# The three-layer feature-crossing tower, staged anew: 32 rounds of 512 columns, and VectorE's share of the low parts contracted in full fp32

## The chip, the core and the metric

One core of one Trainium2 chip runs the whole program. The metric is the device time of one execution in microseconds (us); lower is better. Engines are named as in the profile: PE is TensorE, DVE is VectorE, ACT is ScalarE, POOL is GpSimd, SP is the queue that issues most DMAs.

## The reference

For 1024 rows, 39 table lookups give `e` of 39 fields x 16 numbers. Three layers follow, each over the products of the 39 fields with the state of the layer before (39 fields for layer 0, then 64 rows), and a small dense network on top:

```python
for i, (W, b) in enumerate(zip(Ws, bs)):          # W0: 39*39 x 128; W1, W2: 39*64 x 128
    z = jnp.einsum('bfd,bgd->bfgd', x, h)
    cur = jax.nn.relu(jnp.einsum('bfgd,fgl->bld', z, Wr) + b[None, :, None])
    if i != n - 1:
        h = cur[:, :L // 2]
        direct = cur[:, L // 2:]
    else:
        direct = cur
    outs.append(direct)
return jnp.concatenate(outs, axis=1).sum(-1)
...
h = jnp.maximum(h @ W_top1 + b_top1, 0.0)         # 272 -> 512, with 16 dense columns
h = jnp.maximum(h @ W_top2 + b_top2, 0.0)         # 512 -> 256
y = h @ W_top3
```

All of it is fp32. There are 1024 x 16 = 16384 columns (row, d) in all. Layer 0 uses its symmetry: with the weights of (f,g) and (g,f) added, only 20 cyclic shifts of the fields are needed, three shifts (117 rows) to a tile, which makes 7 tiles. Layers 1 and 2 have 39 x 64 products, which is 19.5 tiles of 128 rows.

## The kernel before

The columns are taken in 16 steps of 1024 (128 batch rows x 8 values of d; `HD`, `N`, `NST`). A unit of work is one tile of 128 (or 117) products by 1024 columns. Its life is: DVE multiplies (`product`, L484 for layers 1 and 2 with h in PSUM and the replicated fields `xr` in SBUF; L474 for layer 0 with both operands in SBUF; L489 for the last half tile), then PE contracts it (`contract`, L712) in one of three ways that `KINDS0` and `KINDS1` write out:

- F: full fp32, two 512-column matmuls, each shown as two records in the profile.
- G: split. ACT copies z to `zh` in fp32r (`hi`, L583), POOL makes `zl = z - zh` (`subtract`, L269), and PE makes three passes of two matmuls each: wl x zh, wh x zh, wh x zl.
- D: the same, but DVE makes `zl` (L502), two units behind its own product (`LAG_SUB`).

A round is layer 0 (7 tiles) of one step, layer 2 (20) and layer 1 (20), 47 units: 20 F, 17 G, 10 D. Two rounds handle one block of 128 rows; PE, DVE, ACT, POOL and SP each run this order in a loop of their own, bound by counting semaphores. The z ring has 6 slots, zh has 5, zl has 3. The half tile of layers 1 and 2 (L723) is done as two 64-row matmuls in different halves of the array.

SP reloads everything replicated from the transposed inputs `xT` in memory: `xk` and `xs` for layer 0 (L359, L364), `xr` and `xl` for layers 1 and 2 (L371, L374), packets of 4 KB. POOL also gathers the embeddings (L255, 39 per block, L252 the ids). PE transposes them (L700), ACT copies the result out and writes `xT` (L594, L598). Sums over d are DVE's (`sum_d`, L511, L515). ACT also makes the relus (`take0`, `take1`, `take2`, L602). The dense network is at the end (`top`, L803, 14 groups), four of its groups before the last layer 2.

## Time and profile before

| | |
|---|---|
| time, median of 3 runs | 1478.6 us (1478.53 to 1479.51) |
| the profiled execution, from its first to its last instruction | 1477.0 us |
| PE matmul busy | 1256.5 us (85%) |
| DVE busy | 1289.5 us (87%) |
| POOL busy | 1052.5 us (71%) |
| ACT busy | 616.3 us (42%) |
| data moved by DMA | 240.57 MB, 163 GB/s |

The profile has no other time for its execution than its span; the runs lie 1.6 us above it in the median, which is what stands outside the first and last instruction. Busy shares are averages over the span, and PE's records overlap in time, so PE's real rate has to be taken from start to start.

### The profile page before, as it was taken

The numbers are of one execution on the slowest core, as the hardware profiler recorded it, in microseconds if no ns is written. First come the engines' busy times: TensorE is split into PE (matmuls) and PEld (weight loads), VectorE is DVE, ScalarE is ACT, GpSimd is POOL, SyncE is SP. The second block draws the span as 40 slices with busy tenths as digits, with TensorE's granted clock in tenths as the row PEclk, the third lists the DMA queues.
The fourth block names the chain that finished last, engine by engine and source line by source line (L and its number), as shares of the span: only waits on it lengthen the run. The fifth ranks groups of instructions, "written<-read, shape, count | busy, mean of one in ns | idle before, by whom it ended". The sixth has DMA issues, their size and how long they took to land.

```text
span 1477.0 us, 15917 instructions
## 1 busy us (share of the span) xinstructions
PE 1256.5 (85%) x4096; PEld 726.8 (49%) x4096; DVE 1289.5 (87%) x1021; ACT 616.3 (42%) x639; POOL 1052.5 (71%) x598
## 2 busy tenths in 40 slices
PE   0057899899988999899988899889988999999999
PEld 0024555455545555455545455555545556555653
DVE  0056989999899999999899999999899999999970
ACT  2122444335353443435443453435444354445442
POOL 6668578885889668894889659895788756555550
PEclk9999999999999999999999999999999999999999
DMA  5189794958769393967949395875949497888600
GB/s 147 21 211 216 169 227 122 212 139 194 179 148 222 100 230 115 210 165 161 223 113 219 100 226 155 175 189 128 227 122 214 123 206 187 176 200 182 136 25 1
DMA packets 89021, 240.57 MB, mean 163 GB/s; under 512 B 21542, under 2 KB 30871, under 8 KB 88888
## 3 DMA queue, kind: packets, MB, share of 16 engines
q1 hardware_dynamic: 77446, 233.70, 67.9%
q0 software_dynamic: 10240, 2.74, 1.7%
q10 hardware_dynamic: 1312, 3.87, 0.9%
q8 instruction: 9, 0.15, 0.0%
q14 instruction: 14, 0.11, 0.0%
HBM read 235.46 MB, written 7.14 MB: 164 GB/s over the span
## 4 chain that ended last, share of the span: by engine, by line
issue 36%; DVE 29%; PE 11%; DMA 7%; POOL 7%; SPq 6%; ACT 2%; DVEq 1%; POOLq 0%; ACTq 0%
DVE z L484 17%; PE curA L712 7%; DVE zl L502 6%; POOL zl L269 5%; DVE z L474 4%; DMA idx<-in_ids_dram 3%; POOL emb L255 2%; SPq L371 2%; DMA xr<-xT 2%; DMA xl<-xT 2%; PE h L803 2%; DVE part L511 1%; PE curB L712 1%; SPq L352 1%; SPq L355 1%
## 5 line engine op out<-in xcount | busy, mean ns | idle before, releaser
L269 POOL TENSOR_TENSOR zl<-z,zh 128x1024 fp32r<-128x1024 f32 (+1 forms) x272 | 668.4, 2459 | 288.9 <-ACT zh L583 263.9
L583 ACT ACTIVATE zh<-z 128x1024 fp32r<-128x1024 f32 (+1 forms) x432 | 455.2, 1058 | 723.0 <-DVE z L484 461.0
L484 DVE TENSOR_TENSOR z<-xr,h 128x1024 f32<-128x1024 f32 x608 | 705.1, 1210 | 53.5 <-PE curA L712 17.7
L255 POOL DMA_INDIRECT emb<-in_tbl_dram,idx x312 | 378.9, 1215 | 97.1 <-issue 61.3
L712 PE MATMUL curA<-z,wf 128*128 128x512 f32 (+1 forms) x592 | 283.4, 601 | 28.6 <-issue 25.3
L502 DVE TENSOR_TENSOR zl<-z,zh 128x1024 fp32r<-128x1024 f32 (+1 forms) x160 | 293.9, 1837 | 5.1 <-ACT zh L583 4.4
L712 PE MATMUL curB<-z,wf 128*128 128x512 f32 (+1 forms) x560 | 267.8, 601 | 4.7 <-DVE z L484 4.7
L712 PE MATMUL curA<-zl,wh 128*128 128x512 f32 (+1 forms) x438 | 148.4, 420 | 70.7 <-POOL zl L269 56.8
L474 DVE TENSOR_TENSOR z<-xk,xs 117x1024 f32<-117x1024 f32 x112 | 193.1, 1773 | 14.3 <-DMA xs<-xT 14.3
L712 PE MATMUL curA<-zh,wl 128*128 128x512 f32 (+1 forms) x438 | 188.2, 511 | 1.4 <-ACT zh L583 1.4
L712 PE MATMUL curB<-zl,wh 128*128 128x512 f32 (+1 forms) x426 | 143.3, 418 | 53.4 <-POOL zl L269 43.8
L712 PE MATMUL curB<-zh,wl 128*128 128x512 f32 (+1 forms) x426 | 182.6, 510 | 1.5 <-ACT zh L583 1.4
L712 PEld LDWEIGHTS curA<-z,wf 128*128 128x128 f32 (+1 forms) x592 | 110.8, 190 | 130.0 <-issue 103.5
L712 PEld LDWEIGHTS curB<-z,wf 128*128 128x128 f32 (+1 forms) x560 | 105.1, 191 | 97.8 <-issue 76.7
L712 PE MATMUL curA<-zh,wh 128*128 128x512 f32 (+1 forms) x438 | 137.1, 394 | 0.0
L712 PEld LDWEIGHTS curA<-zl,wh 128*128 128x128 f32 (+1 forms) x438 | 74.1, 188 | 125.9 <-POOL zl L269 95.7
L712 PE MATMUL curB<-zh,wh 128*128 128x512 f32 (+1 forms) x426 | 133.0, 393 | 0.0
L712 PEld LDWEIGHTS curB<-zl,wh 128*128 128x128 f32 (+1 forms) x426 | 72.2, 188 | 103.7 <-POOL zl L269 78.2
L712 PEld LDWEIGHTS curA<-zh,wl 128*128 128x128 f32 (+1 forms) x438 | 81.8, 190 | 79.1 <-issue 55.3
L712 PEld LDWEIGHTS curB<-zh,wl 128*128 128x128 f32 (+1 forms) x426 | 79.8, 190 | 72.1 <-issue 54.2
L712 PEld LDWEIGHTS curA<-zh,wh 128*128 128x128 f32 (+1 forms) x438 | 82.5, 188 | 18.6
L712 PEld LDWEIGHTS curB<-zh,wh 128*128 128x128 f32 (+1 forms) x426 | 80.2, 188 | 18.4
(60 smaller groups left out, 432.6 us busy)
## 6 DMA issues: line engine op xcount, KB each, us to landing
xr<-xT SPq DMA_DIRECT2D x288, 512.0 KB, 9.3
xs<-xT SPq DMA_DIRECT2D x112, 468.0 KB
xr<-xT SPq DMA_DIRECT2D x32, 256.0 KB
xk<-xT SPq DMA_DIRECT2D x16, 468.0 KB
emb<-in_tbl_dram,idx POOLq DMA_INDIRECT x312
xl<-xT SPq DMA_DIRECT2D x32, 128.0 KB
xT<-direct ACTq DMA_DIRECT2D x16, 156.0 KB
xT<-direct ACTq DMA_DIRECT2D x16, 80.0 KB
```

Of the source, the lines that this page charges most:

```text
L255: nc.gpsimd.indirect_dma_start(out=emb[:, f * D:(f + 1) * D], out_offset=None, in_=tables[f], in_offset=bass.IndirectOffsetOnAxis(ap=idx[: ...
L269: nc.gpsimd.tensor_tensor(zl[0:r, q, :], z[0:r, slot(i), :], zh[0:r, h, :], ALU.subtract).then_inc(lo_pool, 1)
L352: sp.dma_start(stage[0][k:R0:K, t, :], cols).then_inc(w0_loaded, 16)
L355: sp.dma_start(w0t[k:R0:K, t, :], rows).then_inc(w0_loaded, 16)
L371: sp.dma_start(xr[par * H:par * H + H, 2 * q:2 * q + n, :], src).then_inc(xr_loaded[q], 16)
L474: nc.vector.tensor_tensor(z[0:R0, slot(i), :], xk[0:R0, :], xs[0:R0, r, :], ALU.mult).then_inc(z_ready, 1)
L484: ins = nc.vector.tensor_tensor(z[:, slot(i), :], xr[:, t, :], h[:, :], ALU.mult)
L502: nc.vector.tensor_tensor(zl[0:r, q, :], z[0:r, slot(i), :], zh[0:r, h, :], ALU.subtract).then_inc(lo_dve, 1)
L511: nc.vector.tensor_reduce(part[:] if half else zs[:, which, :], src[:].rearrange("p (d b) -> p b d", d=HD), AX.X, ALU.add).then_inc(sum_do ...
L583: nc.scalar.activation(zh[0:r, split_slot(kinds, i, HI_RING), :], z[0:r, slot(i), :], ACT.Copy).then_inc(hi_ready, 1)
L712: mm = nc.tensor.matmul(cur[:, b * BK:(b + 1) * BK], w[0:r, :], v[0:r, b * BK:(b + 1) * BK], start=start_, stop=stop_)
L803: mm = nc.tensor.matmul(cur[0:w.shape[1], cols], w, v, start=(q == 0), stop=(q == len(parts) - 1))
```

## The change

The whole body is rewritten. What it does:

- The columns go in 32 steps of 512 (128 rows x 4 values of d). A unit is now a pair of tiles by 512 columns, so it still has 1024 columns for DVE, ACT and POOL. A round has 24 units: 10 of layer 1, 10 of layer 2 and 4 of layer 0 (the last with one tile), for three different steps. There are 29 full rounds, three before them that lack layers, two after them without layer 0, and a last one with layer 2 alone.
- `KINDS` has F and G only: 15 F (one of them of half size) and 9 G a round. D is used in the rounds before round 0 alone. The half tile is now a second tile of an F unit, with 64 rows: unit 9 ends with it in layer 1, unit 10 begins with it in layer 2, in the other half of the array.
- h is kept in PSUM in two arrangements side by side (`take` makes 6 relus instead of 2), so that one replicated tile `xr` serves two tiles of products: 9 x 256 KB and 512 KB of `xq` are loaded a step, in 14 DMAs of packets of 2 KB.
- For layer 0 the left operand `xk` is no longer loaded: PE transposes the embeddings, copied three times side by side by ACT (`copy_emb`), straight into PSUM (`turn`), where DVE reads it with a stride (`product0`). All of `xs` for a step comes in three DMAs and has one buffer.
- Rings: z 8, zh 4, zl 4. Two embedding buffers. SP writes `xT`. ACT's order inside a round has waits for PE: `take2` at unit 0, `copy_xc` (which waits for `turn` behind PE's unit 1) at unit 2.
- The sums over d stay in SBUF (`zq`, `zs`). Seven of the eight blocks of rows go through the dense network before the last round; the last block follows at the end with 128 columns.

```diff
+DQ = 4
+N = DQ * P
+STEPS = B * D // N
...
+KINDS = "GFGFFGFGFF" + "FGFGFFGFGF" + "FGFF"
+UNITS = len(KINDS)
+A_END, C_END = 10, 20
+FIRST, LAST = -3, STEPS - 1
+LOOP = 8
+LOOPED = (1, 25)
+NZ, NH, NL = 8, 4, 4
...
+def kind(r, u):
+    k = KINDS[u]
+    return "D" if k == "G" and r < 0 else k
...
+            def load_xs(t):
+                for k in range(K):
+                    nt = T0 if k < 2 else T0 - 1
+                    src = bass.AP(xT.tensor, (t * XR + k) * N, [[N, F], [K * N, T0], [1, N]])
+                    sp.dma_start(xs[k * F:(k + 1) * F, :].rearrange("p (t c) -> p t c", c=N), src).then_inc(xs_loaded, 16)
+
+            def load_xr(t, slot, k):
+                for a in range(4):
+                    src = bass.AP(xT.tensor, (t * XR + 12 * k + a) * N, [[0, Q], [4 * N, 3], [1, N]])
+                    sp.dma_start(xr[slot][a * Q:(a + 1) * Q, 3 * k * N:3 * (k + 1) * N].rearrange("p (q c) -> p q c", c=N),
+                                 src).then_inc(xr_loaded[slot][k], 16)
...
+            def round_(r, j=0):
+                t = r + 3
+                if t < STEPS:
+                    sp.wait_ge(xc_copied, t + 1 + LOOP * j)
+                    sp.nop(nofuse=True)
+                    write_x(t + LOOP * j, t % 2)
+                    sp.wait_ge(xT_written[t % 2], 32 * (t // 2 + 1) + 16 * LOOP * j)
+                    sp.nop(nofuse=True)
+                    sp.wait_ge(z_ready, NUM[r - 1, UNITS - 1] + 1 + ZU * j)
+                    sp.nop(nofuse=True)
+                    load_xs(t + LOOP * j)
+                t = r + 2
+                if t < STEPS:
+                    sp.wait_ge(z_ready, NUM[r, A_END] + 1 + ZU * j)
+                    sp.nop(nofuse=True)
+                    load_xq(t + LOOP * j, t % 2)
+                    for k in range(3):
+                        sp.wait_ge(z_ready, NUM[r, A_END + 3 * k + 3] + 1 + ZU * j)
+                        sp.nop(nofuse=True)
+                        load_xr(t + LOOP * j, t % 2, k)
+
...
+            def product1(r, u, j):
+                s = r + 1
+                if u == 0:
+                    dve.wait_ge(read0, 7 * (s + 1) + RU * j)
+                z_free(r, u, j)
+                if u < NQ:
+                    if u % 3 == 0:
+                        dve.wait_ge(xr_loaded[s % 2][u // 3], 64 * (s // 2 + 1) + 32 * LOOP * j)
+                    x = xr[s % 2][:, u * N:(u + 1) * N].unsqueeze(1).to_broadcast([P, 2, N])
+                    pair(x, h1[:, :].rearrange("p (a n) -> p a n", a=2), z_slot(r, u)).then_inc(z_ready, 1)
...
+            def product0(r, u, j):
+                s = r + 3
+                if u == C_END:
+                    dve.wait_ge(turned, s + 1 + LOOP * j)
+                    dve.wait_ge(xs_loaded, 48 * (s + 1) + 48 * LOOP * j)
+                z_free(r, u, j)
+                t = 2 * (u - C_END)
+                nt = tiles_of(u)
+
+                x = xk_bank(s)[0:R0, :].rearrange("p (d b) -> p b d", d=DQ).unsqueeze(1).to_broadcast([R0, nt, P, DQ])
+                nc.vector.tensor_tensor(
+                    z[0:R0, z_slot(r, u), 0:nt * N].rearrange("p (a b d) -> p a b d", a=nt, d=DQ), x,
+                    xs[0:R0, t * N:(t + nt) * N].rearrange("p (a b d) -> p a b d", a=nt, d=DQ),
+                    ALU.mult).then_inc(z_ready, 1)
...
+            def copy_xc(t, j):
+                act.wait_ge(turned, t + 1 + LOOP * j)
+                if t >= 2:
+                    act.wait_ge(xT_written[t % 2], 32 * (t // 2) + 16 * LOOP * j)
+                nc.scalar.activation(xc[t % 2][:, :].rearrange("p (b d) -> p b d", d=DQ),
+                                     xk_bank(t)[0:F, :].rearrange("p (d b) -> p b d", d=DQ), ACT.Copy).then_inc(xc_copied, 1)
...
+            def take(i, h, cur, bias, done, to):
+
+                if i < 2:
+                    relu(h[i * H:(i + 1) * H, 0:N], cur[0:H, :], bias[0:H, :], done)
+                elif i < 6:
+                    p, f = (i - 2) * Q, (i - 1) % 2 * Q
+                    relu(h[p:p + Q, N:2 * N], cur[f:f + Q, :], bias[f:f + Q, :], done)
...
+            def round_(r, j=0):
+                if r == -2:
+                    for i in range(7):
+                        take0(r, i, j)
+                for u in range(UNITS):
+                    if present(r, u):
+                        hi(r, u, j)
+                    if u == 0 and r >= 1:
+                        take2(r - 1, j)
+                    if u == 0 and r >= 1 and (r + 3) % PER_B == 0 and r <= STEPS - 4:
+                        copy_emb((r + 3) // PER_B, j)
+                    if u == 2 and 0 <= r <= STEPS - 4:
+                        copy_xc(r + 3, j)
+                    if u == A_END - 1 and r == -1:
+                        for i in range(7):
+                            take0(r, i, j)
...
+                        take0(r, u - 11, j)
+                    if 0 <= r <= STEPS - 4 and u >= C_END:
+                        for i in range(2 * (u - C_END), min(7, 2 * (u - C_END) + 2)):
+                            take1(r, i, j)
+                    if u == UNITS - 1 and (r == -1 or STEPS - 4 < r <= STEPS - 2):
...
+            def turn(t, b, j):
+
+                ev = emb[b % 2][:, :].rearrange("p (f d) -> p d f", d=D)
+                for c in range(DQ):
+                    mm = nc.tensor.transpose(xk_bank(t)[0:R0, c * P:(c + 1) * P], ev[:, DQ * (t % PER_B) + c, :],
+                                             ident[:, :])
+                mm.then_inc(turned, 1)
+
+            def contract(r, u, j, cur, start, stop):
+                n = tiles_of(u)
+                if kind(r, u) == "F":
+                    pe.wait_ge(z_ready, NUM[r, u] + 1 + ZU * j)
+                    order = (1, 0) if u == A_END else range(n)
+                    for i, a in enumerate(order):
+                        rows = rows_of(u, a)
+                        mm = nc.tensor.matmul(cur[:, :], wf[rows, full_at(u), a, :],
+                                              z[rows, z_slot(r, u), a * N:(a + 1) * N],
+                                              start=start and i == 0, stop=stop and i == n - 1)
+                else:
+                    h, l, w = SNUM[r, u] % NH, SNUM[r, u] % NL, split_at(u)
+                    pe.wait_ge(hi_ready, SNUM[r, u] + 1 + SU * j)
+                    for a in range(n):
+                        rows = rows_of(u, a)
+                        cols = slice(a * N, (a + 1) * N)
+                        nc.tensor.matmul(cur[:, :], wl[rows, w, a, :], zh[rows, h, cols], start=start and a == 0, stop=False)
+                        nc.tensor.matmul(cur[:, :], wh[rows, w, a, :], zh[rows, h, cols], start=False, stop=False)
+                    if kind(r, u) == "G":
+                        pe.wait_ge(lo_pool, POOL_LO[r, u] + 1 + GU * j)
                     else:
...
+                        pe.wait_ge(lo_dve, DVE_LO[r, u] + 1 + DU * j)
+                    for a in range(n):
+                        rows = rows_of(u, a)
+                        mm = nc.tensor.matmul(cur[:, :], wh[rows, w, a, :], zl[rows, l, a * N:(a + 1) * N],
+                                              start=False, stop=stop and a == n - 1)
+                mm.then_inc(z_used, 1)
+
```

## Rows read from the trace of the kernel before

**Rows 1.** The page: busy us, share of the span, instructions.
```profile
PE 1256.5 (85%) x4096; PEld 726.8 (49%) x4096; DVE 1289.5 (87%) x1021; ACT 616.3 (42%) x639; POOL 1052.5 (71%) x598
```

**Rows 2.** Windows, two rounds each: length; busy (records) by engine; clock; DMA share; GB/s.
```profile
624.00:793.50 169.50, 151.75 (x502) 88.15 (x501) 163.31 (x125) 74.13 (x72) 132.84 (x75) 1.00 0.73 172
1216.70:1386.00 169.30, 161.24 (x549) 98.31 (x548) 167.93 (x137) 79.90 (x76) 94.50 (x39) 1.00 0.83 191
```

**Rows 3.** Waits of 624 to 793.5 us: total us, times, longest.
```profile
PEld curA L712 <- POOL zl L269: 15.5, 14, 1.9
DVE z L484 <- PE curA L712: 2.4, 3, 1.5
```

**Rows 4.** Timeline, PE, late stretch without stalls: start us, us, engine, line, operation.
```profile
1419.24 1.88 PE L712 MATMUL curA<-z,wf 128*128 128x512 f32 x4
...
1421.42 0.62 PE L712 MATMUL curA<-zh,wh 128*128 128x512 f32 x2
...
1422.34 1.45 PE L712 MATMUL curA<-z,wf 128*128 128x512 f32 x3
```

**Rows 5.** Timeline, PE, half-tile matmuls and two dense groups.
```profile
1401.18 0.62 PE L712 MATMUL curA<-zl,wh 128*128 128x512 f32 x2
1401.73 1.13 PE L723 MATMUL curA<-z,wf 64*128 64x512 f32 x4
1402.79 6.00 PE L803 MATMUL curB<-xs 128*128 128x512 f32 x12
1408.72 0.70 PE L803 MATMUL h<-xs 128*128 128x512 f32 x1
```

**Rows 6.** Lines L484, L474, L269, L583 and L255 in 624 to 793.5 us: ns min/median/max.
```profile
L484 DVE TENSOR_TENSOR z<-xr,h x77: 1198/1208/1223, 623.6 to 793.0; 128x1024 f32<-128x1024 f32 x77
L474 DVE TENSOR_TENSOR z<-xk,xs x14: 1210/1211/3391, 658.7 to 751.7; 117x1024 f32<-117x1024 f32 x14
L269 POOL TENSOR_TENSOR zl<-z,zh x34: 2370/2386/3242, 624.4 to 789.5; 128x1024 fp32r<-128x1024 f32 x32, 117x1024 fp32r<-117x1024 f32 x2
L583 ACT ACTIVATE zh<-z x54: 1041/1059/1065, 626.0 to 788.5; 128x1024 fp32r<-128x1024 f32 x48, 117x1024 fp32r<-117x1024 f32 x6
L255 POOL DMA_INDIRECT emb<-in_tbl_dram,idx x40: 940/964/1964, 622.6 to 792.1; - x40
```

**Rows 7.** Groups by line: count, busy us, mean ns of one, idle before.
```profile
L502 DVE TENSOR_TENSOR zl<-z,zh 128x1024 fp32r<-128x1024 f32 (+1 forms) x160 | 293.9, 1837 | 5.1 <-ACT zh L583 4.4
L511 DVE TENSOR_REDUCE zs<-direct 128x128 f32<-128x1024 f32 x8 | 15.8, 1978 | 0.0
L511 DVE TENSOR_REDUCE zs<-curB 128x128 f32<-128x1024 f32 x8 | 9.7, 1215 | 0.0
```

**Rows 8.** Timeline, products back to back, and a gather between subtractions.
```profile
587.96 4.60 DVE L484 TENSOR_TENSOR z<-xr,h 128x1024 f32<-128x1024 f32 x4
564.25 0.94 POOL L255 DMA_INDIRECT emb<-in_tbl_dram,idx  x1 [0.30 <-issue]
```

**Rows 9.** Timeline of the start, all engines.
```profile
56.92 1.90 PE L700 MATMUL curA<-ident,emb 128*39 128x128 f32 x8 [56.92 <-DMA emb<-in_tbl_dram,idx]
70.65 1.09 DVE L451 TENSOR_TENSOR xr<-xr 128x896 f32<-128x896 f32 x1 [67.44 <-DMA xr<-w_rows]
74.27 0.63 ACTq L598 DMA_DIRECT2D xT<-direct  x1
77.42 0.86 SPq L359 DMA_DIRECT2D xk<-xT  x1
84.47 1.23 DVE L474 TENSOR_TENSOR z<-xk,xs 117x1024 f32<-117x1024 f32 x1 [7.28 <-DMA xs<-xT]
```

**Rows 10.** DMA of 88 to 120 us, then 1420 to 1430: queue, packets, MB, share.
```profile
q1 hardware_dynamic: 1907, 6.98, 101.6%
...
q1 hardware_dynamic: 816, 0.92, 27.7%
```

**Rows 11.** Timeline of the end.
```profile
1475.36 0.28 SPq L436 DMA_DIRECT2D out_dram<-xr  x1
```

More of the change, by code:

```diff
@@ new lines, in _ @@
+            copy_emb(0, 0)
+            for t in range(3):
+                copy_xc(t, 0)
+            act.wait_ge(small_loaded, 16 * 6)
+            for r in range(FIRST, 1):
+                round_(r)
+            with act.Fori(0, 3) as j:
+                for r in range(1, 1 + LOOP):
+                    round_(r, j)
+            for r in range(LOOPED[1], LAST):
+                round_(r)
+            take2(LAST - 1, 0)
+            act.wait_ge(dense_turned, 1)
+            act.wait_ge(xT_written[0], 16 * STEPS)
@@ L802, in top @@
                 for q, (w, v) in enumerate(parts):
[L803 removed]
+                    mm = nc.tensor.matmul(cur[0:w.shape[1], 0:n], w, v, start=q == 0, stop=q == len(parts) - 1)
                 mm.then_inc(top_done, 1)
[L806 to L810 removed]
```

1096 lines of the change are left out of this document (516 added, 580 removed).

## The prediction, made before the changed kernel had run

> **What bounds the kernel now.** I read the busy line first: DVE 87%, PE 85%, POOL 71% of the whole span [rows 1]. These are averages with a start and an end in them, so the second view is two windows of two rounds each. In 169.5 us DVE is busy for 163.3 us (96%), PE's records for 151.8 us, POOL for 132.8 us; without gathers POOL falls to 94.5 us, the length stays at 169.3 us and DVE is at 167.9 us [rows 2]. So DVE is the bound; POOL is not, or the later window would be shorter. PE's records overlap. Its real rate comes from starts: an F unit and a G unit take 3.10 us together, from one z,wf start to the next (1419.24 to 1422.34). The last two passes of G take 0.92 us by starts (1421.42 to 1422.34), so a G unit is 3 x 0.46 = 1.38 us, and an F unit is 1.72 us [rows 4]. Of the 94 units of two rounds 40 are F (4 of them the half tile, about 1.15 us from rows 5) and 54 are G or D: 36 x 1.72 + 4 x 1.15 + 54 x 1.38 = 141 us, with 16 transposes (1.90 us for 8 in rows 9) 145 us, 85% of 169.5. PE has 24 us of slack in two rounds, and the waits agree: PE waits for single low parts, 1.1 us each, and DVE almost never for PE [rows 3]. One odd row matters later: DVE operations with both operands in SBUF have a long tail beside POOL (L474 median 1211 ns, maximum 3391; L502 mean 1837), those with one operand in PSUM have none (L484 1198 to 1223) [rows 6, 7].
>
> **The change: the steady rounds.** 1024 columns are now two rounds of 24 units, 48 for the former 47.
>
> PE. Layers 1 and 2 of a round have 12 F and 8 G: 12 x 1.72 + 8 x 1.38 = 31.7 us. Layer 0 has 2.5 F and 1 G: 4.3 + 1.4 = 5.7 us [rows 4]. The two half tiles now meet at the border of layers 1 and 2, in different halves of the array and different banks. The four records of two such matmuls took 1.06 us from their start to the next matmul's, where one alone would take 0.86 [rows 5]. I take one of the two 0.86 us as hidden and 0.3 us for switching to half tiles and back (the start at 1401.73 is 0.09 us late after 2 x 0.23, and 1.06 is 0.20 over 0.86): -0.56. Four transposes: 0.95, half of 1.90 [rows 9]. Sum 31.7 + 5.7 - 0.6 + 0.95 = 37.8 us; I use 37.9 a round. The two rounds are 75.8 us, for 145/2 = 72.5 us of PE work and 84.7 us of length before. So the change adds some 3 us of PE work per 1024 columns and can win only because DVE's share was longer.
>
> On the switch the Trainium skill (TensorEngine Tiling (Array Packing), Key Properties) has a rule that speaks against half tiles: changing the tiling mode drains the engine, while tiles within one mode run independently. Two dense groups agree with the drain: 12 records with a 16-row matmul in each half take 5.93 us where 12 x 0.43 is 5.16 [rows 5], 0.19 us a switch. By the rule the sum would be what I have.
>
> DVE. A product is 1.15 us in a row of four (4.60/4) [rows 8]: 23 x 1.15 + 0.6 for the half unit = 27.1. The 10 subtractions of a former round, 1.84 us each [rows 7], are gone. Layer 0's products now have their left operand in PSUM with a stride. The nearest rows are a strided PSUM reading by a reduction, 1215 ns for 1024 columns, and L474 at 1211 [rows 6, 7]; bounds 1.15 and 1.98 (the strided SBUF reduction), taken 1.2, as the PSUM row is nearest. Sums over d: two of 512 columns a round, and half of one more: 0.6 to 1.0 us each, 2.5 taken. DVE has 29 to 33 us in 37.9: hidden, cover at least 5 us.
>
> POOL. 9 subtractions of 2.386 us and 39/4 gathers of 0.964 + 0.30 us [rows 6, 8]: 21.5 + 12.3 = 33.8 us. Hidden, but with only 4.1 us of cover.
>
> ACT. 9 copies of 1.06 [rows 6], 15 relus of half that width, 0.6 each, 0.6 for `copy_xc`, 0.3 for `copy_emb`: 19.4 us. What counts is the order. `take2` sits at ACT's unit 0 and waits for PE's unit 19 of the round before; `copy_xc` at unit 2 waits for `turn` behind PE's unit 1. Queued behind the second are `hi` of units 5 and 7, and behind these POOL. From the end of `turn`, PE works through units 2, 3 and 4 (1.38 + 1.72 + 1.72 = 4.8 us) and the first two thirds of unit 5 (0.92) before it needs unit 5's low part at 5.7 us; it comes at 0.6 + 1.06 + 2.39 = 4.1 us, with semaphores 4.3. Unit 7: POOL has one gather (1.1 us) between, so 4.3 + 3.5 = 7.8 us; needed at 5.7 + 0.46 + 1.72 + 0.92 = 8.8. For unit 11 it is 12.5 to 14.8, for 21 28.5 to 30.6. Each is in time, by 1.0 us at the least. With DVE faster than PE it runs 8 slots ahead (12 us), which is what makes this hold.
>
> SP and DMA. A step loads 2.36 MB of `xr`, 0.52 of `xq`, 1.68 of `xs`: 4.6 MB in 37.9 us is 120 GB/s, for 172 before. The queue delivered 6.98 MB in 32 us, 218 GB/s, when full [rows 10]: 21 us, hidden. `xs` has one buffer: `write_x` (3.2 us to landing, 74.27 to 77.42 in rows 9), then 3 DMAs, in all about 12 to 15 us after `turn`; DVE wants it about 18 us after, and PE 28.
>
> **The change: start and end.** The 39 serial loads of W0 become 6 DMAs, so the sum at 70.65 us is no longer what the start waits for; the gathers are (transposes at 56.92) [rows 9]. From there: copy of the embeddings 1.3 us, first `turn` 0.9, copy 0.6, write and landing 3.2 = 63 us. First product: 7.05 us from the load for 0.94 MB before [rows 9], now 1.68 MB: 10 us, so 73 us against 84.5. Then loads set the pace, at 218 GB/s: xq and xr of step 0 13 us, xs of step 1 7 (it stands behind them in SP's order), xr of step 1 13, xs of step 2 7. Layer 0 of step 1 at 91 us, layer 1 of step 0 at 97, ready to begin round 0 at 123. There the relus of both layers (14 x 0.6, partly side by side with PE) and the first low parts come late: 127 us. A second batch of gathers ends by 57 + 39 x 1.25 = 106 us, slower in parts, still in time.
>
> Sum: round 0 begins at 127; 29 rounds x 37.9 = 1099; two rounds without layer 0 and transposes, 31.1 each: 62. Before the last round 14 dense groups: 4 of 2.97 and 4 of 2.3 (384 columns), 3.4 x 2 + 2.6 x 2, 3.0, plus 8 transposes and ACT's copies 3 and small waits 1: 41. Last layer 2: 16. The end (relu 0.6, two reductions 1.3, 12 + 8 + 2 matmuls of 128 columns with their relus about 5, and 1.7 from the last DMA's issue at 1475.36 to the end [rows 11]): 9. Together 127 + 1099 + 62 + 41 + 16 + 9 = 1354 us of span. The old span of 1477.0 us was 1.6 below the median, so 1355.6, say **1356 us**, 8.3% faster.
>
> **The rivals.**
>
> A: the half tiles do not run side by side. There is now a wait (`z_ready`, `read1`) between them where before there was none. 0.86 us x 31 borders = 27 us: 1383.
>
> B: the low parts come late. POOL's cover of 4.1 us and the 1.0 us of unit 7 are thin, and a gather reached 1964 ns and a subtraction 3242 [rows 6]. If a round costs POOL's 33.8 plus stalls of 6 to 7 us behind ACT's two waits, it takes 40 to 41 us: 29 x 2.1 to 3.1 = 61 to 90 us more, 1417 to 1446. For it speaks that PE waited for POOL 14 times in two rounds on one bank alone, with slack [rows 3]; against it the times worked out above.
>
> C: slower. Everything outside the 29 rounds is 255 us, so the change loses once a round takes (1477 - 255)/29 = 42.1 us. The one mechanism that gets there is POOL slowed at the port that it shares with DVE: at the maxima of its rows a round would be 9 x 3.24 + 9.75 x 2.26 = 51 us, and the time 255 + 1480 = 1735. Place: `subtract` on POOL beside `product1` and `product2`. Against it: POOL's median is 2386 ns beside L484, whose form most new products have, and the long rows go with L474 and L502, both of which vanish. The Trainium skill (SBUF — State Buffer, Who interferes with whom) says the same: a DVE instruction with at most one SBUF input, outside the two-port modes, does not contend with GpSimd. The trace agrees: L484 never left 1198 to 1223 ns.
>
> D: packets have a fixed price. They shrink from 4 KB to 2 KB. With 1907 packets in 32 us on 16 queues a packet took 0.27 us [rows 10]; at that price 2230 a step are 38 us, DMA becomes the bound at 39 a round, and the start is 40 us longer: about 1427. Against it: 816 packets of 1.1 KB took 0.054 us each (27.7% of 16 x 10 us), so time goes with bytes.
>
> **How the numbers follow.** Forecast 1356: 0.62. A: 0.15. B: 0.15. D: 0.03. C: 0.05. The start and end are uncertain by 15 us, the round by -0.3 to +0.4 us (9 to 12 us) in the likeliest case: 1335 to 1376. The range goes on to A and into the lower part of B: 1335 to 1412. Faster by over 0.2% (about what a measurement of this kernel can tell from no change): 0.94; within 0.2%: 0.01; slower: 0.05.
>
> **What would show it.** Two rounds 75 to 77 us apart; in them PE's idle time in single waits of under 1 us, DVE busy about 80% and waiting for PE; POOL near 89%, its subtractions at 2.39 us without a tail; layer 0's product at 1.21 us; DMA near 155 MB. The 64-row records side by side or one after the other decides A. First product at 73 us, round 0 at 127 us. The prediction is wrong if PE waits for POOL or ACT in most rounds by more than 1 us (B), if POOL's subtraction exceeds 2.5 us (C), or if products wait for `xs` (D).

## The result, and the profile of the changed kernel

| | before | after |
|---|---|---|
| time, median of 4 runs | 1479.05 us (1478.53 to 1481.08) | **1375.1 us** (1373.74 to 1377.09) |
| ratio, 95% interval | | 0.930 (0.928 to 0.932) |
| span of the profiled execution | 1477.0 us | 1372.1 us |
| data moved by DMA | 240.57 MB | 160.45 MB |

The change makes the kernel 7.0% faster. The forecast was 1356 us, 19 us too low, inside its range of 1335 to 1412.

The busy line of the changed kernel, which answers to [rows 1] (busy us, share of the span, instructions):

```profile
PE 1256.9 (92%) x3852; PEld 707.1 (52%) x3852; DVE 944.1 (69%) x876; ACT 661.5 (48%) x879; POOL 973.8 (71%) x607
```

DVE has fallen from 87% to 69% and PE has risen to 92%. Three windows of 76 us, two rounds each (length; busy with records by engine PE, PEld, DVE, ACT, POOL; clock; DMA share; GB/s), answer to [rows 2]:

```profile
408.00:484.00 76.00, 76.00 (x236) 43.32 (x235) 58.31 (x54) 39.92 (x51) 62.89 (x39) 1.00 0.70 131
700.00:776.00 76.00, 76.00 (x236) 43.14 (x235) 59.00 (x55) 39.97 (x52) 62.91 (x40) 1.00 0.70 128
1000.00:1076.00 76.00, 76.00 (x237) 43.47 (x236) 59.37 (x55) 39.78 (x51) 62.88 (x39) 1.00 0.71 130
```

PE has no idle time left. DVE has 17 us to spare in 76. Some of the rows that say who waits for whom, from 180 to 1240 us (total us, times, longest), answer to [rows 3]:

```profile
POOL zl L261 <- ACT zh L607: 180.5, 55, 7.0
DVE z L474 <- PE curM L757: 104.4, 159, 1.5
DVE z L514 <- DMA xs<-xT: 48.3, 26, 3.3
PEld curM L774 <- POOL zl L261: 1.4, 2, 0.9
PE curM L774 <- POOL zl L261: 0.5, 1, 0.5
```

The direction has turned: DVE now waits for PE 159 times, where before it was PE that waited for low parts. PE waits for POOL in three rows over 28 rounds. The third row is one of the signs by which the prediction said it could be told to be wrong: products do wait for `xs`, in 26 places. More on that below. The length of a round is read from the transposes, which come once a round; these are those of rounds 0 and 28:

```profile
155.73 0.87 PE L746 MATMUL xk<-ident,emb 128*117 128x128 f32 x4
1210.30 0.87 PE L746 MATMUL xk<-ident,emb 128*117 128x128 f32 x4
```

(1210.30 - 155.73)/28 = 37.66 us. The kernel before took 169.5/4 = 42.4 us for the same 512 columns [rows 2]. Of the 28 rounds 26 take 37.54 to 37.58 us. The other two take 38.8 and 38.9; they are those that cross from one pass of the hardware loop of 8 rounds to the next. Durations in the steady part (ns min/median/max) answer to [rows 6]:

```profile
L474 DVE TENSOR_TENSOR z<-xr,h x508: 1204/1215/1224, 180.4 to 1239.3; 128x1024 f32<-128x1024 f32 x170
L514 DVE TENSOR_TENSOR z<-xk,xs x112: 679/1215/1226, 213.0 to 1233.1; 117x1024 f32<-117x1024 f32 x84, 117x512 f32<-117x512 f32 x28
L261 POOL TENSOR_TENSOR zl<-z,zh x254: 2347/2392/2441, 178.3 to 1237.2; 128x1024 fp32r<-128x1024 f32 x112, 117x1024 fp32r<-117x1024 f32 x15
```

The long tails are gone on both engines: every product now has an operand in PSUM, and the longest of 254 subtractions on POOL took 2.44 us, where one before took 3.24.

The start is where time was lost. ScalarE and then PE of the changed kernel (start us, us, engine, line, operation, idle before and its releaser), which answer to [rows 9]:

```profile
85.63 1.06 ACT L607 ACTIVATE zh<-z 117x1024 fp32r<-117x1024 f32 x1 [10.43 <-issue]
117.23 4.00 ACT L624 ACTIVATE h<-curY,bias 64x512 f32<-64x512 f32 x6 [30.54 <-remote]
```

```profile
89.99 2.74 PE L757 MATMUL curY<-z,wf 117*128 117x512 f32 x6
111.41 3.78 PE L757 MATMUL curM<-z,wf 117*128 117x512 f32 x4 [18.68 <-issue]
```

PE ends the first layer 0 at 89.99 + 2.74 = 92.7 us; the relus (`take0`), which wait for nothing else in the program, start at 117.23. The first product came at 83.18 us, round 0 on PE at 150.90. In the kernel before, the first relu followed PE's last matmul of layer 0 at once (row in the last section).

### The profile page after: what moved, and what is told of

It is laid out like the page before. It is cut to its first block, busy times and chain, and to the rows that moved or that the text cites. A ratio compares the mean times of both kernels' runs of the same rounds, so it can differ in the third digit from the quotient of the medians.

```text
span 1372.1 us, 14847 instructions
## 1 busy us (share of the span) xinstructions
PE 1256.9 (92%) x3852; PEld 707.1 (52%) x3852; DVE 944.1 (69%) x876; ACT 661.5 (48%) x879; POOL 973.8 (71%) x607
## 2 busy tenths in 40 slices
DMA packets 101047, 160.45 MB, mean 117 GB/s; under 512 B 17322, under 2 KB 29467, under 8 KB 100845
## 3 DMA queue, kind: packets, MB, share of 16 engines
q0 software_dynamic: 10240, 2.74, 1.9%
## 4 chain that ended last, share of the span: by engine, by line
PE 86%; issue 5%; POOL 4%; another core or an unknown queue 3%; ACT 1%; DMA 1%; DVE 0%; POOLq 0%; DVEq 0%; ACTq 0%
PE curM L757 45%; PE curY L757 9%; PE curM L766 8%; PE curM L774 8%; PE curM L767 8%; POOL emb L250 3%; PE h L842 2%; PE xk L746 1%; POOL zl L261 1%; PE curY L767 1%; PE curY L766 1%; PE curY L774 1%; PE curY L842 1%; PE xk L842 1%
## 5 line engine op out<-in xcount | busy, mean ns | idle before, releaser
L261 POOL TENSOR_TENSOR zl<-z,zh 128x1024 fp32r<-128x1024 f32 (+1 forms) x281 | 668.7, 2386 | 308.5 <-ACT zh L607 254.0
L474 DVE TENSOR_TENSOR z<-xr,h 128x1024 f32<-128x1024 f32 x576 | 676.5, 1217 | 215.9 <-PE curM L757 137.9
L757 PE MATMUL curM<-z,wf 128*128 128x512 f32 (+2 forms) x1546 | 693.7, 599 | 18.7 <-issue 18.7
L607 ACT ACTIVATE zh<-z 128x1024 fp32r<-128x1024 f32 (+1 forms) x288 | 300.7, 1054 | 293.0 <-DVE z L474 189.6
L757 PEld LDWEIGHTS curM<-z,wf 128*128 128x128 f32 (+2 forms) x1546 | 275.6, 189 | 291.7 <-issue 262.2
L766 PE MATMUL curM<-zh,wl 128*128 128x512 f32 (+1 forms) x514 | 295.1, 574 | 9.7 <-ACT zh L607 7.9
L767 PE MATMUL curM<-zh,wh 128*128 128x512 f32 (+1 forms) x514 | 202.3, 394 | 0.0
L774 PE MATMUL curM<-zl,wh 128*128 128x512 f32 (+1 forms) x514 | 160.0, 393 | 1.9 <-POOL zl L261 1.9
L757 PE MATMUL curY<-z,wf 117*128 117x512 f32 x310 | 145.2, 598 | 16.8 <-issue 16.8
L766 PEld LDWEIGHTS curM<-zh,wl 128*128 128x128 f32 (+1 forms) x514 | 97.6, 190 | 78.9 <-issue 42.3
L624 ACT ACTIVATE h<-curY,bias 64x512 f32<-64x512 f32 (+1 forms) x186 | 120.2, 646 | 35.2 <-remote 30.5
L624 ACT ACTIVATE h<-curM,bias 32x512 f32<-32x512 f32 (+1 forms) x198 | 127.9, 646 | 9.7 <-DVE z L474 2.9
L474 DVE TENSOR_TENSOR z<-xq,h 128x1024 f32<-128x1024 f32 x64 | 75.3, 1217 | 14.5 <-PE curM L757 14.5
```

What stands on the lines that cost most here:

```text
L261: nc.gpsimd.tensor_tensor(zl[0:n, SNUM[r, u] % NL, :], z[0:n, z_slot(r, u), :], zh[0:n, SNUM[r, u] % NH, :], ALU.subtract).then_inc(lo_poo ...
L474: return nc.vector.tensor_tensor(z[:, slot, :].rearrange("p (a n) -> p a n", a=2), x, h, ALU.mult)
L607: nc.scalar.activation(zh[0:n, SNUM[r, u] % NH, :], z[0:n, z_slot(r, u), :], ACT.Copy).then_inc(hi_ready, 1)
L624: nc.scalar.activation(dst, src, ACT.Relu, bias=bias).then_inc(done, 1)
L757: mm = nc.tensor.matmul(cur[:, :], wf[rows, full_at(u), a, :], z[rows, z_slot(r, u), a * N:(a + 1) * N], start=start and i == 0, stop=stop ...
L766: nc.tensor.matmul(cur[:, :], wl[rows, w, a, :], zh[rows, h, cols], start=start and a == 0, stop=False)
```

## The experiments

All were timed beside the kernel before on the same chip, in several rounds, unless it is said otherwise. They ran in four groups, each on a chip of its own: D made F, two D, and the two on the loads; one G more, the half tiles, the gathers held and the single column; the split gathers, three D and both together; the split gathers again. Since chips turned out to differ at the start, steady rounds are compared by their length, read as above from the transposes of rounds 0 and 28.

### The kernel before, with D made F and nothing else

```diff
-KINDS0 = "FDFGFDF"
-KINDS1 = "FGDFGFGDFGFGDFGFGDGF"
+KINDS0 = "FFFGFFF"
+KINDS1 = "FGFFGFGFFGFGFFGFGFGF"
```

> The kernel before, with its D units turned into F and nothing else. Theory (what made the gain is VectorE's relief, the new staging is not needed for it): two rounds become bound by TensorE, 56 x 1.72 + 4 x 1.15 + 34 x 1.38 + 3.8 = 152 us for 169.5, 8 pairs save 110 to 140 us: 1340 to 1370 us. Rival (the old rings of 6 and 3 slots and the old order let TensorE wait for POOL's low parts, so the staging is what cashes the relief): above 1420 us, with the waits of TensorE for POOL grown from 41 us in two rounds or kept.

Measured: 1386.38 us (1385.38 to 1391.34), ratio 0.9375 (0.934 to 0.941). A window of 300 us in the middle, of the kernel before and then of this one:

```profile
600.00:900.00 300.00, 268.89 (x893) 156.79 (x891) 289.32 (x224) 132.32 (x129) 231.62 (x129) 1.00 0.77 179
```

```profile
600.00:900.00 300.00, 293.84 (x890) 159.93 (x889) 242.10 (x201) 103.33 (x101) 239.71 (x142) 1.00 0.80 187
```

DVE's share falls from 96% to 81% and PE's rises to 98%. Its transposes of one kind stand at 333.06 and, five blocks of 2048 columns on, at 1108.85, which is 38.8 us per 512 columns for 42.4. The time lies between the theory's range and the rival's, nearer to the first: one edit of two strings gives 92.7 of the 104 us. The rival's sign did not come: the rows in which PE or its weight loads wait for POOL sum to 48 us from 300 to 1200 us, where the kernel before has 217. In steady rounds the new staging is worth another 38.8 - 37.7 = 1.1 us per 512 columns, some 36 us over 32 (an estimate from these two lengths). Only 11 us of it are left in the time; the rest goes in the start, the end and the rounds that lack layers.

### The changed kernel with two D

```diff
-KINDS = "GFGFFGFGFF" + "FGFGFFGFGF" + "FGFF"
+KINDS = "GFGFDGFGFF" + "FGFGDFGFGF" + "FGFF"
```

> Two F units of a round (units 4 and 14) become D: VectorE makes their low parts again. Theory (the rounds are bound by TensorE, VectorE and the POOL port have room): each D unit saves 1.72 - 1.38 = 0.34 us of TensorE, 0.68 us a round, about 21 us in 31 rounds: 1354 us, rounds of 37.0 us. Rival (the two subtractions, with both operands in SBUF, take the port that POOL reads through, and low parts come late): VectorE subtractions of 2 us and more, POOL subtractions above 2.6 us, rounds of 38 us or longer and 1375 to 1400 us.

Measured: 1362.75 us (1361.69 to 1364.04), ratio 0.922 (0.919 to 0.925): 12 us faster than the changed kernel. This kernel has the new rounds and most of the step from D to F: of the 10 low parts per 1024 columns that DVE made in the kernel before, it makes 4 again. It is 116 us faster than the kernel before. So making all ten F, worth 93 us in the old rounds, goes too far in the new ones: the last four cost 12 us. The unit prices say 21 us (2 x (1.72 - 1.38) = 0.68 a round); the round fell only from 37.66 to (1200.73 - 154.50)/28 = 37.37. Its chain of work (share of the span by engine) and its largest wait of PE for another engine from 180 to 1240 us:

```profile
PE 48%; POOL 24%; issue 20%; another core or an unknown queue 3%; DVE 2%; ACT 2%; DMA 0%; POOLq 0%; DVEq 0%; ACTq 0%
```

```profile
PEld curM L774 <- POOL zl L261: 20.9, 53, 0.6
```

PE's weight loads wait 53 times for a low part, where the changed kernel has 2 such waits. In the last rounds, which have no gathers, the transposes stand at 1126.78 and 1163.74, 36.96 us apart, which is what the prices say. So the missing 0.4 us a round is POOL. The rival's prices did not come: DVE's subtraction has a median of 1226 ns, POOL's 2386 and a maximum of 2524. Single operations do have long tails again, though: one DVE subtraction took 3393 ns and one gather 1774 (992 at most in the changed kernel). What share of POOL's lateness they have was not separated.

### One G more in place of an F

```diff
-KINDS = "GFGFFGFGFF" + "FGFGFFGFGF" + "FGFF"
+KINDS = "GFGFFGFGGF" + "FGFGFFGFGF" + "FGFF"
```

> The changed kernel with one more of its 24 units split in three cheap contractions with the low part by GpSimd instead of contracted in full fp32 (10 G and 14 F a round instead of 9 and 15). TensorE's round falls by 0.34 us (1.72 - 1.38) to 37.3, GpSimd's rises from 33.8 to 36.2. If TensorE's work is the bound and GpSimd keeps up with 1 us to spare: 1375 - 29 x 0.34 = 1365. If GpSimd's low parts come late, since its gathers stand between them: TensorE waits for GpSimd some 1 to 3 us a round and the time is 1400 or more.

Measured: 1393.38 us (1391.22 to 1395.16), ratio 0.942 (0.937 to 0.946): 18 us slower, between the two times of the expectation and nearer to the rival's. Four transposes of it, two with gathers beside them and two behind the last gather:

```profile
928.38 0.87 PE L746 MATMUL xk<-ident,emb 128*117 128x128 f32 x4
966.80 0.87 PE L746 MATMUL xk<-ident,emb 128*117 128x128 f32 x4
...
1120.68 0.87 PE L746 MATMUL xk<-ident,emb 128*117 128x128 f32 x4
1157.92 0.87 PE L746 MATMUL xk<-ident,emb 128*117 128x128 f32 x4
```

38.4 us with gathers, 37.2 without. The second is the price of the arithmetic (37.3); the first is POOL (a window of just under two such rounds):

```profile
408.00:484.00 76.00, 74.14 (x235) 42.92 (x234) 57.94 (x54) 41.07 (x52) 65.81 (x40) 1.00 0.68 124
```

POOL's records fill 65.8 of 76 us, and a gap of 0.30 us before each gather belongs to its cost (19.5 gathers in two rounds, 5.9 us). That is 94% of a window that the stalls have stretched. Set against what PE needs, POOL has some 36.2 us of work for a round of 37.2, 97%, and that stalled PE by 1.2 us a round. With 9 G the same sum is 62.9 + 5.9 = 68.8 us of 76, 91%, and PE waits for nothing; so the cover was as thin as the forecast had it. Where the tenth G stands, right behind another, may add to it; that was not separated.

### Three D, eight G

```diff
-KINDS = "GFGFFGFGFF" + "FGFGFFGFGF" + "FGFF"
+KINDS = "GFGFDFGFGF" + "FGFGDFGFGF" + "FDFF"
```

> The changed kernel with three units whose low part VectorE subtracts (two that were contracted in fp32, one that was GpSimd's): 8 G, 3 D and 13 F a round. TensorE's arithmetic is that of the kernel with two D (37.0 us a round by the unit prices, 37.4 measured, 1362.8 us), GpSimd's falls from 33.8 to 31.4 us, VectorE's rises by 1.2 us. If the 0.4 us a round that the kernel with two D lies above its sum are GpSimd's late low parts (20.9 us of waits in 53 places), this one takes 37.0 a round: 1362.8 - 28 x 0.4 = 1352. If they are TensorE's own or ScalarE's high parts, it takes 1360 to 1365.

Measured: **1338.28 us** (1337.58 to 1338.84), ratio 0.9093 (0.9075 to 0.911), the kernel before at 1472.14 beside it. Besides the third D, two G of the first layer in the order stand one place later than in the kernel with two D; what that does by itself was not separated. The transposes:

```profile
142.40 0.87 PE L746 MATMUL xk<-ident,emb 128*117 128x128 f32 x4
1177.92 0.87 PE L746 MATMUL xk<-ident,emb 128*117 128x128 f32 x4
```

The round is (1177.92 - 142.40)/28 = 36.98 us, the 37.0 that the prices give, and the waits of PE for POOL are gone (2.8 us in four places). That is 0.4 a round, 11 us, below the kernel with two D, as the first theory had it. The time lies 14 us below the 1352 of the expectation. Some 12 us of that (round 0 stands at 142.4 where the other had 154.5) came with the chip and not from the edit, as the start's runs below make likely. This version beats both kernels: by its round, 28 x (37.66 - 36.98) = 19 us faster than the changed one, the chip's start left aside. The changed kernel with its gathers in two parts (below), on the same chip, is 22 us slower than this one.

### The half tiles with a full tile between them

```diff
-                    order = (1, 0) if u == A_END else range(n)
+                    order = range(n)
```

> The changed kernel with the two half tiles at the seam of layers 2 and 1 issued in their stored order, so that two products of the same 64 rows of the array follow one another instead of two of different rows. What the order of the half tiles is worth: the trace of the changed kernel has 12 dense products there in 4.7 us against 5.16 for 12 full ones, so about 0.47 us a round, 31 rounds, 15 us: 1389. Rival: the halves overlap little, or the order does not matter, since the waits around them are longer: 1375 to 1378.

Measured: 1413.52 us (1410.03 to 1415.91), ratio 0.956 (0.951 to 0.960): 38 us slower, 1.25 a round (155.65 to 1245.11 us for 28 rounds, 38.91). The expectation had 15 us. It also describes the edit wrongly: with the stored order, unit 10 does its full tile first, so a full tile stands between the two halves. PE around the border of the two layers, of the changed kernel and then of this one (12 dense records, and the second matmul of the G unit behind them; its first one starts early or late by 0.3 us, by what stands ahead of it, and is no good mark):

```profile
505.12 4.85 PE L757 MATMUL curM<-z,wf 128*128 128x512 f32 x12
...
510.04 0.39 PE L767 MATMUL curM<-zh,wh 128*128 128x512 f32 x1
```

```profile
516.42 5.90 PE L757 MATMUL curM<-z,wf 128*128 128x512 f32 x12
...
522.59 0.40 PE L767 MATMUL curM<-zh,wh 128*128 128x512 f32 x1
```

4.92 us against 6.17, which is the 1.25 us a round. What full tiles take there shows in one and in two F units without halves, a little later in the changed kernel:

```profile
511.19 1.88 PE L757 MATMUL curM<-z,wf 128*128 128x512 f32 x4
...
513.13 0.39 PE L767 MATMUL curM<-zh,wh 128*128 128x512 f32 x1
...
514.27 3.59 PE L757 MATMUL curM<-z,wf 128*128 128x512 f32 x8
...
517.93 0.40 PE L767 MATMUL curM<-zh,wh 128*128 128x512 f32 x1
```

To the same mark one takes 1.94 us and two take 3.66, so three would take 5.38. Take it that a half costs a full tile's 0.86 us. Apart, the array goes from full to half and back twice: four switches for 6.17 - 5.38 = 0.79 us, 0.20 each. Side by side, one 0.86 is hidden and there are two switches: 5.38 - 0.86 + 2 x 0.20 = 4.92, which is what was measured. The 0.20 is near the 0.19 that the prediction worked out of [rows 5]. The Trainium skill (TensorEngine Tiling (Array Packing), Key Properties) says that a change of the tiling mode drains the engine; by that rule too the halves belong next to each other, and these two traces agree.

### The order of the loads at the start

```diff
-            load_xq(0, 0)
-            for k in range(3):
-                load_xr(0, 0, k)
...
             load_xs(1)
-            load_xq(1, 1)
+            load_xq(0, 0)
             for k in range(3):
-                load_xr(1, 1, k)
+                load_xr(0, 0, k)
...
+            load_xq(1, 1)
+            for k in range(3):
+                load_xr(1, 1, k)
```

> At the start SP loads xs of step 1 ahead of xq and xr of step 0, and xs of step 2 ahead of xq and xr of step 1. Theory (the 24 us that the start was longer than predicted is loads in that order, at a lower rate than assumed): the second layer-0 group of products starts near 97 instead of 110 us, round 0 on TensorE near 135 to 140 instead of 151 us, 1360 to 1365 us. Rival (ScalarE's first relus, at 117 us, are what the start waits for, and not by the loads' order): the relus stay at 115 us or later, and the time at 1372 us or more.

Measured: 1372.33 us (1371.06 to 1373.61), ratio 0.928 (0.925 to 0.931), not to be told from the changed kernel by the intervals, as the rival had it. The second step's layer 0 came 11 us earlier (99.15 for 110.13), but the relus in front of it on ScalarE stayed late:

```profile
99.15 4.08 DVE L514 TENSOR_TENSOR z<-h,xs 117x1024 f32<-117x1024 f32 x4 [13.99 <-issue]
```

```profile
115.28 4.01 ACT L624 ACTIVATE h<-curY,bias 64x512 f32<-64x512 f32 x6 [31.88 <-remote]
```

### The same order, with the large loads held until layer 0

```diff
+            sp.wait_ge(read0, 7)
             load_xq(0, 0)
```

> As the run with the loads reordered, and xq and xr of step 0 are issued only when ScalarE's seven relus of step 0 are through. If ScalarE's relus waited for its instructions behind the bulk loads (they were ready at 93 us and began at 117 us, one instruction packet landed in between), they now begin near 93 to 98 us. If they are late for another reason, they begin at 115 us or later and the time grows by some 15 us over the reordered kernel.

Measured: 1383.51 us (1380.89 to 1383.88), ratio 0.935 (0.932 to 0.939). The relus start at 113.73, although SP's queue has issued nothing between 86 and 118 us. So the loads do not hold them up. Nor does the fetch of instructions: no packet of an instruction queue landed between 86 and 114 us. Holding the loads costs 11 us over the reordered kernel (8 over the changed one), since layer 1 now waits for `xr` (6.5 us before DVE's product at 127.25).

### The second group of gathers held until layer 0

```diff
+            pool.wait_ge(read0, 7)
+            pool.nop(nofuse=True)
             pool.wait_ge(idx_loaded[1], 16)
             for f in range(F):
                 gather(f, 1)
```

> The second group of 39 gathers, which GpSimd issues from 58 to 105 us in the changed kernel, waits for the first seven activations of layer 0 instead (read0 >= 7) and so runs from about 100 to 150 us; nothing else is altered. In four kernels of the new staging ScalarE's first activation of layer 0 starts 8 to 12 us after GpSimd's last gather (105.4 to 117.2, 104.8 to 115.3, 105.2 to 115.0, 105.6 to 113.7), although TensorE had finished what it needs by 93. Theory: the stream of gathers holds it up; then the activation starts at 93 to 95, the first product of layer 1 comes at about 115 (held by the second set of loads) instead of 124.2, and the kernel takes 5 to 10 us less (1365 to 1370). Rival: the gathers have nothing to do with it; the activation starts at 113 to 118 as before, GpSimd's gathers then run to about 165, its first low part (151 us) is some 15 us late and so is the round, 1385 to 1395.

Measured: 1373.55 us (1372.17 to 1375.71), ratio 0.929 (0.925 to 0.933), no change in the time, though the relus come 27 us earlier:

```profile
89.72 4.00 ACT L626 ACTIVATE h<-curY,bias 64x512 f32<-64x512 f32 x6 [5.86 <-PE curY L759]
```

```profile
150.02 1.22 PE L776 MATMUL curM<-zl,wh 128*128 128x512 f32 x2 [12.23 <-POOL zl L261]
```

The releaser of the relu has a name again, PE's layer 0. What was won went into a new wait: POOL's gathers now run to 147.6 us, and PE waits 12.23 us for POOL's first low part. The theory is right in that the gathers have a part in the delay, and wrong on the gain (it said 1365 to 1370); the late low part that the rival foretold came as well.

### A single column ahead of the late activation (one run)

```diff
                 if r == -2:
+                    relu(probe[0:H, :], ident[0:H, 0:1], bias0[0:H, :], probed)
                     for i in range(7):
                         take0(r, i, j)
```

> The changed kernel with one activation more on ScalarE: a Relu of 64x1 into a scratch column, which waits for nothing, directly ahead of the first activation of layer 0. If that activation stands at 117 us because its semaphore is late (it waits for TensorE's count), the one of a single column runs at about 87, right after ScalarE's copy at 85.63. If ScalarE itself stands still (its instructions, or the first Relu), the single column also comes at about 117. The time is that of the changed kernel, 1374 to 1377, either way, unless the stall is a fixed cost of the first Relu that is then paid earlier: then the activation of layer 0 starts at about 93 plus nothing and the kernel gains up to 7 us.

Measured: 1378.23 us, one run.

```profile
82.13 0.28 ACT L626 ACTIVATE probe<-ident,bias 64x1 f32<-64x1 f32 x1
114.62 4.00 ACT L626 ACTIVATE h<-curY,bias 64x512 f32<-64x512 f32 x6 [32.21 <-remote]
```

ScalarE runs a Relu at 82.13 and then stands for 32 us before the next one. The next one is larger and reads PSUM, but what it has to wait for is PE's count, and PE was done at 88.5. So it is not the first Relu that costs the time, and ScalarE was still at work at 82 us; what ends late is the wait for the count. That ScalarE as a whole stood still from then on is not excluded by this run alone. Its rounds took 37.9 us, which makes up the 3 us by which it lies above the changed kernel; why was not followed up.

### The gathers in two parts

```diff
+            pool.wait_ge(xc_copied, 3)
+            pool.nop(nofuse=True)
             pool.wait_ge(idx_loaded[1], 16)
             for f in range(F):
+                if f == 12:
+                    pool.wait_ge(read0, 7)
+                    pool.nop(nofuse=True)
                 gather(f, 1)
```

> The changed kernel with the second group of 39 gathers in two parts: 12 of them from when ScalarE has copied the third transpose (about 66 us), the other 27 from when ScalarE has made layer 0 of step 0 (about 94 us), so that they end at about 128 us, before GpSimd's first low part is due at 147. With all 39 held back, layer 0 came at 89.7 instead of 117.2, and TensorE was ready for round 0 at about 135, but then waited 12.2 us for GpSimd, whose gathers ran to 147.6. Theory (a stream of gathers delays ScalarE's wait, and a stream that ends early enough costs nothing): layer 0 at 90 to 95, round 0 at about 138, the time 1375 - 12 = 1363. Rival: what delays the activation is not the gathers but where the profile happens to stand, or the 12 gathers suffice for it: layer 0 again after 105, the time 1372 to 1376.

Measured: 1359.97 us (1357.81 to 1362.48), ratio 0.925 (0.923 to 0.927), the kernel before at 1472.14 beside it; relus at 86.74, round 0 on PE at 134.51. It looks like the theory come true. But the kernel with three D, whose gathers are not held, ran on the same chip, and there:

```profile
86.88 4.00 ACT L624 ACTIVATE h<-curY,bias 64x512 f32<-64x512 f32 x6 [5.89 <-PE curY L757]
```

```profile
103.79 0.94 POOL L250 DMA_INDIRECT emb<-in_tbl_dram,idx  x1 [0.30 <-issue]
```

The gathers run to 104.7 us and the relus are on time. This chip does not have the delay at all, so the 15 us are mostly the chip's. The changed kernel itself was not run on such a chip.

### Three D, gathers in two parts, and the new order of the loads

```diff
-KINDS = "GFGFFGFGFF" + "FGFGFFGFGF" + "FGFF"
+KINDS = "GFGFDFGFGF" + "FGFGDFGFGF" + "FDFF"
...
+                if f == 12:
+                    pool.wait_ge(read0, 7)
+                    pool.nop(nofuse=True)
                 gather(f, 1)
...
             load_xs(1)
+            load_xq(0, 0)
...
```

> Three D as in the kernel beside it, the gathers in two parts as in the other, and the loads of the start in the order that brings the second step's layer-0 factors first. If the gains are independent: 1352 - 12 - 2 = 1338; if the start's gain is given back in the first rounds (round 0 bound by VectorE, whose ring is empty at its start, or by the loads), 1345 to 1352.

Measured: 1336.61 us (1334.77 to 1338.6), ratio 0.9086 (0.9065 to 0.9107). Against three D alone on the same chip (1338.28) that is 1.7 us and not to be told from nothing by the intervals. The traces have round 0's transposes at 139.0 and 142.4. So on a chip without the delay the two edits of the start are worth some 3 us at most. That the time meets the 1338 of the expectation is luck: the 14 us that it gives to the start's two edits came with the chip.

### The gathers in two parts, on another chip

The edit is that of the gathers in two parts, unaltered.

```diff
+                if f == 12:
+                    pool.wait_ge(read0, 7)
```

> The kernel with the gathers in two parts, once more. The three kernels of the last group ran on a chip on which the activation of layer 0 came without delay in all of them, also in the one whose gathers were not held (86.9 us, with the gathers running to 104.7), and ScalarE's copies of the weights were done at 32 us instead of 51 to 55; the kernel before took 1472 us there and 1479 on the others. So what they say of the start is what that chip does, not what the gathers' place does. Theory: the delay belongs to some chips and to the stream of gathers together; on such a chip (the kernel before at about 1479) the split brings layer 0 at 90 to 95 and 1360 to 1366. Rival: 12 gathers ahead of the activation suffice to bring the delay back: layer 0 after 105, 1372 to 1376. On a chip without it (the kernel before at about 1472) the run repeats 1360 and decides nothing.

Measured: 1360.54 us (1358.49 to 1362.85), ratio 0.925 (0.923 to 0.927), the kernel before at 1471.57. A second chip without the delay (relus at 88.12), so it repeats the number and decides nothing, as the expectation had said for such a chip. Whether the split helps on a chip with the delay was not seen.

## Why the prediction was right, and where its 19 us went

**Direction and mechanism: right.** DVE was the bound, PE is now. Windows, waits and the chain (PE is 86% of the span in it) show what was foretold. The number owes something to luck: the start's term was 24 us too low and other terms 9 us too high.

**PE's round.** 37.9 forecast, 37.66 measured. Over 29 rounds that is 7 us less than in the sum. The halves side by side save 0.46 us in the trace, 0.56 in the sum; the rest of the difference is some 0.01 us in the price of each of 24 units. The 37.66 is a mean that has the two long rounds in it.

**The others.** DVE 58.31 x 37.66/76 = 28.9 us a round (forecast 29 to 33); ACT 19.8 (19.4); POOL 31.2 of records and 2.9 of gaps, 34.1 (33.8); layer 0's product 1.215 us (1.2); 160.45 MB (155). POOL's cover held, with one more G it did not. What did not hold is the time of `xs`. The prediction gave 12 to 15 us from `turn` to its landing and 18 to DVE's need of it. In the round at 418.74 us DVE's first product of layer 0 came 18.3 us behind `turn` (419.61 to 437.94) and had waited the last 1.9 of them for `xs`. So the sign that it set for rival D came, by a later landing and an earlier need, without rival D: DVE's slack and its lead over PE took these waits, up to 3.3 us, and PE has no wait for them.

**The terms of the sum.** Middle and end: dense groups 1308.12 to 1346.86, 38.7 us (41); last layer 2 16.1 (16); end 9.1 (9). Start: round 0 at 150.90 for 127, **the term that failed**, by 24 us. The rounds gave 7 us back and the dense groups 2; the two rounds without layer 0 took 65 us (62). Together 24 - 7 + 3 - 2 = 18, the span's 1372 for 1354. The median lies 3 us above the span, where the forecast had added 2.

The step was "Then loads set the pace, at 218 GB/s", and round 0 at 127 from it. On the two chips without the delay nearly the same start gives 134.51 and 135.56 (gathers in two parts, one on each) and 137.57 (three D), so 7 to 11 us were missed by the sum itself. In the first of these the first product came at 77 us for 73 and the second layer 0 at 102 for 91, both waiting for `xs`, and layer 1 at 107 for 97, right behind the second on DVE; 218 GB/s was the best rate of a full queue [rows 10], and the changed kernel's start ran at 190 in the mean from 80 to 125 us. The remaining 13 to 16 us are the late wait on ScalarE and the chip's slower start around it; their shares were not separated. Nothing in [rows 9] could show them: in the kernel before, ScalarE's first relu followed PE's last matmul of layer 0 at once, at 103.17 us.

**Rival A** (halves not side by side, 1383): refuted by the trace, 4.92 us with the halves side by side against 6.17 apart. Its price was too low: 0.86 us a border, where 1.25 a round was lost and the kernel took 1413.5, since the switches double as well (0.86 + 2 x 0.20 = 1.26). **Rival B** (late low parts): did not happen with 9 G, and is what happens with 10, though for less: 38.4 us a round, where it had 40 to 41. **Rival C** (POOL slowed by DVE): refuted, 2.39 us in the median and 2.44 at the most. **Rival D** (a fixed price of a packet): refuted, the DMA share is 0.70 in a steady window, where 1.0 was its claim, though the packets are 2 KB.

**What the prediction left out** is that the two parts of the change are not worth their sum. F for all ten D in the old rounds brings 93 us; the new rounds with four of the ten left bring 116, with none left 104. I had priced D to F as PE time that DVE's relief pays for. In the new rounds, where DVE has 8 us of 38 to spare, the last units had nothing left to pay for: 15 F and 9 G cost 37.66 where 13 F, 8 G and 3 D cost 36.98. The new rounds with all ten D per 1024 columns were not run. By their prices, an estimate, DVE would have 28.9 + 5 x 1.23 = 35.0 us a round and PE 37.7 - 5 x 0.34 = 36.0, so that DVE might already be off the bound without any F in place of D.

## What to carry to other kernels

When a change has two parts that relieve the same engine, price the second on the profile that the first would leave: here F for D was worth 93 us alone, and behind the other part its last four units of ten cost 12. When an engine is the bound, look first at which work can go to the one with slack, and by how much that one may be filled: POOL with work for 91% of PE's round, issue gaps counted, stalled nobody, with 97% it cost 1.2 us a round. And before a gain at the start is believed, compare kernels on the same chip.

## What the hardware showed that was not expected

**Chips differ in the start.** On the chips of the first two groups ScalarE's copies of the weights ended at 51 to 55 us (so too in the profile of the changed kernel above), on the two others at 32 to 33. A row of each (the changed kernel with two D; three D):

```profile
50.83 0.31 ACT L585 ACTIVATE wf<-xs 78x128 f32<-78x128 f32 x1 [1.48 <-issue]
```

```profile
31.69 0.69 ACT L585 ACTIVATE wf<-xs 117x128 f32<-117x128 f32 x3
```

The first have gaps of mostly 1.1 us, up to 1.8, between copies before which the profile names no wait; the second have none. The kernel before takes 1479 us on the one sort and 1472 on the other. The rounds are the same on both (37.66 and 37.68 us for the arithmetic of the changed kernel).

**Beside a stream of gathers, on a chip of the first sort, a wait can end far too late.** In the five kernels in which it was followed, ScalarE's wait for PE's count ended 8 to 12 us after the last of 39 gathers and 23 to 26 us after PE had done its work. With the gathers held back, on such a chip, it ended at once, and with the gathers running, on a chip of the second sort, it did too. It is not this count alone. ScalarE's third copy of `xc`, which waits for a DMA's write, shows it in the changed kernel, and not with the gathers held (7.04 us of idle time for 1.44):

```profile
74.61 0.59 ACT L620 ACTIVATE xc<-h 39x512 f32<-39x512 f32 x1 [7.04 <-remote]
```

```profile
65.89 0.59 ACT L622 ACTIVATE xc<-h 39x512 f32<-39x512 f32 x1 [1.44 <-DMA xT<-xc]
```

PE's first transposes wait for ScalarE's copy of the embeddings. In the changed kernel they start 6.7 us after it ends, with the gathers held 3.6 us, on the second sort of chip 0.15 us; so some of the lateness needs no gathers:

```profile
56.94 1.24 ACT L612 ACTIVATE emb<-emb 128x1248 f32<-128x1248 f32 x1 [1.66 <-DMA emb<-in_tbl_dram,idx]
64.92 1.18 PE L746 MATMUL xk<-ident,emb 128*117 128x128 f32 x4 [64.92 <-remote]
```

And the two together are not enough. The kernel before, in a profile with the same gaps between the copies, has gathers until 102.8 us, and its first relu comes at once when PE is done:

```profile
101.25 1.88 PE L712 MATMUL curA<-z,wf 117*128 117x512 f32 x4
101.85 0.94 POOL L255 DMA_INDIRECT emb<-in_tbl_dram,idx  x1 [0.30 <-issue]
103.17 2.18 ACT L602 ACTIVATE h<-curA,bias 64x1024 f32<-64x1024 f32 x2 [5.54 <-PE curA L712]
```

By what path the gathers delay a wait, and what else it takes, was not settled.

**A half tile between full ones** costs some 0.86 us, as a full tile does, and 0.40 us of switching (twice 0.20); two halves of different rows next to each other cost 0.86 + 0.40 together.
